# The last stage of a fused transformer-like block on one core: routing put beside the next pair's first logits, gate term held in PSUM, outputs written tile by tile

## The reference, cut to what matters

```
x = x + attention(layernorm(x), ctx)
x = x + lora_ffn(layernorm(x), ...)
h = layernorm(x)
x = x + (mask * h * A_S1 + (1 - mask) * h * A_S2)      # channel attention, mask from ctx
h = layernorm(x)
logits = h @ router_weight.T + router_bias             # 64 experts
scores = softmax(logits);  topk_w = top 8 of scores
w_dense = scores where among the top 8, else 0
x = x + (h * sum(topk_w) + w_dense @ expert_bias)
```

## Time and profile before

| | us |
|---|---|
| median of 3 runs | 4076.12 |
| lowest, highest of the runs | 4073.73, 4076.64 |
| the profiled execution: time | 4075.54 |
| the profiled execution: span of its trace | 4074.0 |
| expert stage in that trace (first matmul at 3506.5) | 567.5 |

### The profile page before, as it was taken

One profiled execution on the slowest core, in us unless ns is written; L12 is line 12 of the kernel. 1 busy time (PEld: TensorE's weight loads), 2 busy tenths in 40 slices (PEclk: granted clock), 3 DMA queues, 4 the chain that ended last, 5 costly groups with the idle time before them and its releaser, 6 DMA issues. The chain is left out here.

```text
span 4074.0 us, 52120 instructions
## 1 busy us (share of the span) xinstructions
PE 3533.0 (87%) x14366; PEld 1876.7 (46%) x14366; DVE 2914.6 (72%) x6957; ACT 1990.7 (49%) x5301; POOL 1740.0 (43%) x1103
## 2 busy tenths in 40 slices
PE   5999999999999995999999989989999960377777
PEld 3666666666666663444443434444444430122222
DVE  3777777777777763368888897879798887365654
ACT  4445444544454431445646474655655553443431
POOL 4777767767777662003131311304040313154544
PEclk9999999999999997999999999999999985677776
DMA  4333333333333224444536353545444431334342
GB/s 158 119 106 122 111 106 126 106 114 121 123 126 110 85 66 149 117 126 131 164 104 191 104 166 100 164 121 166 126 148 146 122 96 52 127 114 164 115 155 83
DMA packets 415676, 504.14 MB, mean 124 GB/s; under 512 B 19350, under 2 KB 349465, under 8 KB 392505
## 3 DMA queue, kind: packets, MB, share of 16 engines
q1 hardware_dynamic: 394076, 392.22, 30.9%
q10 hardware_dynamic: 9824, 71.34, 4.7%
q0 software_dynamic: 11520, 37.76, 2.8%
HBM read 370.16 MB, written 131.10 MB: 123 GB/s over the span
## 5 line engine op out<-in xcount | busy, mean ns | idle before, releaser
L887 PE MATMUL acc<-xh,ws 128*128 128x512 f16 x4096 | 1238.2, 390 | 87.7 <-DVE xr L1384 84.1
L887 PE MATMUL acc<-xl,ws 128*128 128x512 f16 x2048 | 775.7, 388 | 3.4 <-DVE xl L1191 3.4
L887 PEld LDWEIGHTS acc<-xh,ws 128*128 128x128 f16 x4096 | 406.3, 100 | 644.5 <-issue 132.4
L1041 ACT ACTIVATE unused<-ct,minus_guess 128x256 bf16<-128x256 f32 x1024 | 505.1, 494 | 342.1 <-DVE minus_guess L1259 254.5
L796 POOL DMA_DIRECT2D ct<-ctx_pairs x128 | 71.1, 556 | 1044.6 <-DVE mk L1309 1035.2
L390 PE MATMUL bu<-m_iz,zf 128*128 128x256 f32 x2048 | 457.2, 382 | 11.8 <-issue 11.8
L390 PEld LDWEIGHTS bu<-m_iz,zf 128*128 128x128 f32 x2048 | 392.2, 192 | 94.0 <-issue 43.1
L887 PEld LDWEIGHTS acc<-xl,ws 128*128 128x128 f16 x2048 | 204.0, 100 | 260.0 <-issue 23.3
L316 POOL TENSOR_TENSOR xt<-xt 128x512 f32<-128x512 f32 x64 | 81.0, 1266 | 375.6 <-ACT xt L496 375.6
L409 PE MATMUL bx<-m_ic,pf 128*128 128x256 f32 x1024 | 234.3, 382 | 3.8 <-POOL pf L248 3.8
L358 PE MATMUL by<-cx,m_k 128*128 128x512 f32 x512 | 231.6, 595 | 2.6 <-DMA cx<-ctx 2.6
(11 more groups left out here) (260 smaller groups left out, 7522.6 us busy)
## 6 DMA issues: line engine op xcount, KB each, us to landing
ws<-w_split SPq DMA_DIRECT2D x128, 1024.0 KB, 5.4
xn<-x SPq DMA_DIRECT2D x16, 2048.0 KB, 7.6
cx<-ctx SPq DMA_DIRECT2D x64, 512.0 KB, 5.1
xt<-xT SPq DMA_DIRECT2D x64, 512.0 KB, 3.9
x_pairs<-xo SPq DMA_DIRECT2D x64, 512.0 KB, 3.2
ct<-ctx_pairs POOLq DMA_DIRECT2D x128, 256.0 KB, 3.7
xn_pairs<-xr ACTq DMA_DIRECT2D x32, 1024.0 KB, 4.8
x<-xn_pairs SPq DMA_DIRECT2D x32, 1024.0 KB, 4.9
```

The costliest lines, as they stand in the source:

```text
L887: product = lambda k, a, x, start: pe.matmul(acc[b][:], ws[o % WR][:, k, a, :], x[:, k, :], start=start, stop=False)
L1041: act.activation(signs[:, u // 2, t] if n == COUNTS - 1 else unused[u % 2][:], ct[k % CR][:, t], ACT.Sign, bias=guess[q % 2][:, u:u + 1], ...
```

## The change

Only `experts_phase` is changed.

1. `x3` is done in halves (128x1024) and its sum goes to a PSUM tile `up` and no longer back to `gc`. The multiplication then reads one operand from PSUM and one from SBUF.
2. The ring `po` has 3 buffers of one tile (128x512); biases and outputs go tile by tile, 16 instructions a pair on DVE for 8 before. The PSUM tiles `tr` and `ab` become one, `rw_ps`, which also takes the transposed weights.
3. The first two chunks of the *next* pair's `x3` are made early on DVE: two halves among the outputs, two within `routing`. PE does the logits of those chunks and the squares of chunk 0 between the transposes of `lgs` and `weights`.
4. The order on PE is a row of small groups (3 biases, 2 squares, 4 logits, and so on), and ACT squares chunk 0 and 1 of the next pair before `weights`.
5. There are 3 buffers `sq`, and POOL halves chunks 0 and 1 of the next pair after the products.
6. SP loads `xr` of the next pair chunk by chunk, each behind the products that used its buffer, and stores a chunk of the pair before after each load, one pair earlier in its program than before.

The diff, cut to what sets the order:

```diff
-    RING = 2
+    RING = 3
-        sq = [sb(f"sq3_{i}", [P, CK, T]) for i in range(2)]
+        sq = [sb(f"sq3_{i}", [P, CK, T]) for i in range(NCH - 1)]
-        lw, tr, ab, dev = pb("lw", [P, 512]), pb("tr", [P, 512]), pb("ab", [P, 512]), pb("dev3", [P, 512])
-        po = [pb(f"po{i}", [P, HK, T]) for i in range(RING)]
+        lw, rw_ps, dev, up = pb("lw", [P, 512]), pb("rw_ps", [P, 512]), pb("dev3", [P, 512]), pb("up", [P, HK, T])
+        po = [pb(f"po{i}", [P, T]) for i in range(RING)]
...
@@ SP, pair(i, s, u)
+                for c in range(NCH):
+                    if not is_last(i):
+                        if least(i, 1):
+                            n_used = counted(sp, NH * (i - 1) + CH * (c + 1))
+                            sp.wait_ge(k_in, 96)
+                            sp.wait_ge(prod_ok, n_used)
+                        load_x(i + 1, 1 - s, c)
+                    if least(i, 1):
+                        n_out = counted(sp, KT * (i - 1) + CK * (c + 1))
+                        sp.wait_ge(k_in, 96)
+                        sp.wait_ge(out_ok, n_out)
+                        store(i - 1, c)
...
@@ POOL
             def pair(i, s, u):
-                for c in range(NCH):
-                    halve(i, c)
+                for h in range(NH):
+                    if h in (2, 5):
+                        halve(i, 2 + h // 4)
                     if least(i, 1):
-                        products(i, 1 - s, c)
+                        product(i, 1 - s, h)
+                if not is_last(i):
+                    halve(i + 1, 0)
+                    halve(i + 1, 1)
...
@@ PE
+            def bias(i, s, u, k):
+
+                if k >= RING:
+                    pe.wait_ge(out_ok, KT * (i - 1) + k - RING + 1)
+                elif least(i, 2):
+                    pe.wait_ge(out_ok, KT * (i - 1))
...
+                pe.matmul(po[(KT * s + k) % RING][:], eb[:, k * P:(k + 1) * P], wds[s][:], start=True, stop=True).then_inc(bias_mm, 1)
...
+                biases(0, 1, 2)
+                squares(i, 1)
+                logits(i, s, 2)
+                biases(3, 4, 5)
+                logits(i, s, 3)
+                if not is_last(i):
+                    deviation(i + 1, 1 - s, u + s)
+                squares(i, 2)
+                biases(6, 7, 8)
+                squares(i, 3)
+                biases(9, 10, 11, 12, 13, 14, 15)
+                pe.wait_ge(lg_ok, i + 1)
...
                 for q in range(QT):
                     mm = pe.transpose(raw[:, q, :], lgs[:, q * P:(q + 1) * P], ident[0:A, 0:A])
                 mm.then_inc(tr_mm, 1)
                 if not is_last(i):
-                    deviation(i + 1, 1 - s, u + s)
-                if least(i, 1):
-                    biases(i, 1 - s, u + s - 1, 2)
-                    biases(i, 1 - s, u + s - 1, 3)
+                    logits(i + 1, 1 - s, 0)
+                    logits(i + 1, 1 - s, 1)
+                    squares(i + 1, 0)
                 weights(i, s)
...
@@ ACT, pair(i, s, u)
+                squares(i, s, 2)
+                if follows:
+                    act.wait_ge(mk_in[1 - s], 16 * (u + s + 1))
+                    gates(i + 1, 1 - s, 0)
+                squares(i, s, 3)
+                if follows:
+                    gates(i + 1, 1 - s, 1)
+                act.wait_ge(lg_mm, i + 1)
...
+                act.activation(lgs[:], lw[0:A, :], ACT.Copy).then_inc(lg_ok, 1)
+                if follows:
+                    gates(i + 1, 1 - s, 2)
+                    squares(i + 1, 1 - s, 0)
+                    gates(i + 1, 1 - s, 3)
                 act.wait_ge(var_ok, i + 1)
                 act.activation(r4[:], r4[:], ACT.Sqrt, bias=eps[:]).then_inc(std_ok, 1)
                 act.wait_ge(arg_ok, i + 1)
                 act.activation(sc[:], lt[:], ACT.Exp).then_inc(exp_ok, 1)
+                if follows:
+                    squares(i + 1, 1 - s, 1)
                 act.wait_ge(wt_mm, i + 1)
...
@@ DVE
+            def x3(i, s, u, h):
+                c, k = h // CH, slice(h * HK, (h + 1) * HK)
...
+                dve.tensor_tensor(up[:], gc[c][:, h % CH * HK:(h % CH + 1) * HK, :], dev[:].unsqueeze(1).broadcast_to([P, HK, T]), ALU.add).then_inc(u_ok, 1)
...
+                dve.tensor_tensor(xr[s][:, k, :], up[:], xr[s][:, k, :], ALU.mult).then_inc(x3_ok, 1)
...
+                o = ost[k // CK][:, k % CK, :]
+                dve.tensor_tensor(o, o, po[(KT * s + k) % RING][:], ALU.add).then_inc(out_ok, 1)
...
                 dve.tensor_tensor(lt[:], raw[:, :, 0:E], lm[:], ALU.subtract).then_inc(step_ok, 1)
+                if not is_last(i):
+                    x3(i + 1, 1 - s, u + s, 2)
                 dve.wait_ge(step_ok, n + 4)
...
                 dve.tensor_tensor(lt[:], lt[:], bc(mx), ALU.subtract).then_inc(arg_ok, 1)
+                if not is_last(i):
+                    x3(i + 1, 1 - s, u + s, 3)
                 dve.wait_ge(exp_ok, i + 1)
...
+                x3(i, s, u, 4)
+                x3(i, s, u, 5)
+                x3(i, s, u, 6)
+                outputs(0, 1, 2)
+                x3(i, s, u, 7)
+                outputs(3, 4, 5, 6)
+                ahead(0)
+                outputs(7, 8, 9)
+                ahead(1)
+                outputs(10, 11, 12, 13, 14, 15)
+                routing(i, s, u)
```

More of the change, by code:

```diff
@@ L1847, in _ @@
             for k in range(KT):
[L1848 removed]
+                mm = pe.matmul(rw_ps[:, 0:E], ones[:], rt[:, k, 0:E], start=k == 0, stop=k == KT - 1)
             mm.then_inc(rsum_mm, 1)
@@ L1899, in pair @@
-            def pair(i, s, u):
-                for c in range(NCH):
-                    logits(i, s, c)
-                    if c:
-                        squares(i, c - 1)
-                    if c in (1, 2) and least(i, 1):
-                        biases(i, 1 - s, u + s - 1, c - 1)
-                squares(i, NCH - 1)
-                pe.wait_ge(lg_ok, i + 1)
-                if least(i, 1):
-                    pe.wait_ge(wd_ok, i)
+                pe.matmul(rw_ps[:], pick[0:A, :], wds[s][0:A, :], start=True, stop=True).then_inc(ab_mm, 1)
@@ new lines, in pair, with biases @@
+            def pair(i, s, u):
+                earlier = least(i, 1)
+                def biases(*tiles):
+                    if earlier:
+                        for k in tiles:
+                            bias(i, 1 - s, u + s - 1, k)
+                biases(0, 1, 2)
[10 more added lines that the diff above has]
+                pe.wait_ge(lg_ok, i + 1)
+                if earlier:
+                    pe.wait_ge(a1_ok, i)
@@ L1966, in weights @@
                     act.wait_ge(prod_ok, NH * (i - 1))
[L1967 to L1983 removed]
+                act.activation(a1[s][:], rw_ps[:], ACT.Identity, bias=ones[:, 0:1]).then_inc(a1_ok, 1)
             act.wait_ge(mk_in[0], 16)
```

187 lines of the change are left out of this document (77 added, 110 removed).

## The result

| | before | after |
|---|---|---|
| median, us | 4076.38 (4 runs) | 3940.98 (4 runs) |
| lowest, highest | 4073.73, 4078.88 | 3939.08, 3953.02 |
| the profiled execution: time, span | 4075.54, 4074.0 | 3939.08, 3937.5 |

The account below looks back on a forecast made before the run. No engine was full; each 68.4 us pair was a ring of waits, PE its largest part. 3567.0 (first pair) + 6 x 49 + 41 (last) + 36.8 (tail) = 3938.8 of span, so 3940 us; forecast range 3924 to 3955, chance 0.60.

Parts of the forecast that it names:

- PSUM gate term: In `x3` on DVE: the sum in PSUM removes the collision with POOL, so a half takes 2.5 us, not 3.5.
- the first pair: Start of the expert stage: ACT's gates and squarings set it, routing ends at 3567.0 us, no gain over 3566.4.
- (a): Routing's end to `weights`: four logits and two squares stand ahead on PE, 7.5 us from cold, so `weights` starts 2.9 later.
- (b): `weights`: PE comes to it warm, so it takes 2.4 us where it took 4.0 at 1.2 GHz.
- (c): PE from `weights` up to bias 6: 20 matmuls at 0.86 us, 17.2 us, with no lasting wait inside.
- (d): DVE from bias 6 to routing: ten outputs and two halves of `x3`, 12.0 us, the seven last biases keeping pace.
- (e): Routing on DVE with two halves of `x3` inside: 13.0 us and 0.1 of hand-offs, square root ready just in time.
- allowance for the clock: Added to each pair: 1.4 us, as three last biases at half clock cost 2.6, taken half the time.
- The first (no cold start): Rival: PE does not go cold in the routing gap; pair 45.3 us, total 3916; chance 0.08.
- The second (the clock falls again during `weights` and the first biases): Rival: PE falls to 1.2 GHz a second time each pair; pair 54.3 us, total 3977; chance 0.22.
- The third: Rival: DVE's collision with POOL stays; pair 51.6 us, last pair 43, total 3958; chance 0.05.
- The fourth: Rival: PE never regains full clock in its small groups; pair 76.4 us, total 4130, slower; chance 0.03.

Follow-up runs that it names:

- no_hole: The kernel after with deviation one group earlier, both `x3` halves placed around output 6, and ACT's last gates behind the exponential: 3933.92 us, ratio 0.965.
- after_again: The kernel after, unedited, timed again on the same chip beside `no_hole`: 3942.52 us, ratio 0.967.
- gate_sbuf: The kernel after with the sum of gate and deviation written back to its SBUF tile: 3973.13 us, ratio 0.974.
- early_dev: The kernel after with the next pair's deviation one group earlier on PE and its first `x3` half ahead of output 6 on DVE: 3942.84 us, ratio 0.966.
- no_hole_busy_pe: `no_hole` with three filler matmuls, results unread, ahead of PE's second group of logits: 3929.95 us, ratio 0.964.

## Why the prediction was right

The mechanism held: the gain is the order's. All pieces in the old order gave about 4 us, and a warm `weights` in the old order none. Taking the PSUM gate term out of the new order costs 25 to 32 of the 136 us, so some 100 are the order with the other pieces. Which of its moves gives how much was not separated, but for the place of `weights`.

That the total is right to 1 us is luck. In the profiled execution the first pair ended 7.6 us later than forecast, the six steady pairs took 5.3 us less, the last pair 3.0 less and the tail 0.5 less, and these nearly cancel.

By steps, from the timeline above, for the long and the short pair:

| step | predicted | pair to 3721.1 | pair to 3767.4 | mean of six |
|---|---|---|---|---|
| (a) end of routing to `weights` | 2.9 | 1.35 | 0.05 | 0.9 |
| (b) `weights` | 2.4 | 2.5 | 2.5 | 2.5 |
| (c) PE up to bias 6 | 17.2 | 17.5 | 17.6 | 17.5 |
| (d) DVE from bias 6 to routing | 12.0 | 14.2 | 11.7 | 12.8 |
| (e) routing with two halves | 13.1 | 14.3 | 14.4 | 14.4 |
| allowance for the clock | 1.4 | in (d) | in (d) | in (d) |
| sum | 49.0 | 49.8 | 46.2 | 48.1 |

**(a) and (e)** were each off, and the errors offset each other, in part from one cause. The six matmuls took 7.5 us in the pair that ended at 3671 (3665.11 to 3672.64), as predicted, with the clock back 4.7 us after their start (0.52 in the window from 3666, so 0.16 of its 4 us at full clock, and 1.00 in the next). But routing is 1.3 us longer than forecast, because of the select steps: 2.97 us for four where `no_hole` has 1.25. POOL halves a chunk beside them. The select steps stand behind the last half of `x3`, so routing ends 6.2 us behind that half and not 4.6, and since PE has its six matmuls at that time, `weights` waits less by as much. The rest of the miss in (a) is that PE idled less before the second group than the "some 5 us", 2.7 to 3.9 us in five of six pairs, and needed less than 7.5 us in those pairs. The prediction looked for the collision on `x3` and products only; its halving "beside routing" was to cost nothing. In one pair of the six, the one that ended at 3721, PE idled just 2.75 us before its second group of logits and did them in 3.65; in the five others they took 5.01 to 5.98.

**(c)** was right to 0.4 us, and DVE's wait of 5.95 and 6.05 for bias 6 was the "some 6 us".

**(d)** is where long and short pairs differ. The hole of 1.20 us before the last three biases, which wait for an output behind `ahead(1)`, is in all six. In the three long pairs the clock falls to 0.50 during it or within 0.5 us behind it, and the three biases take 5.04, 5.49 and 5.49 us; in the three short ones 2.84, 3.09 and 3.28. Over 2.74 at full clock that is 1.5 us a pair, where the allowance was 1.4: "three biases at half clock cost 2.6, taken half the time". That the sizes agree so well is luck too, since nothing in the prediction says when the clock falls. Long and short pairs alternate in this trace, but `after_again`, the same kernel, has 47.4, 49.6, 49.6, 49.2, 46.7 and 46.9.

**The PSUM gate term**: 2.5 for a half was right (1.225 and 1.224 and the hand-offs). By the rule of the Trainium skill (SBUF — State Buffer, "SBUF: two separate sides") an operation of VectorE with at most one input in SBUF stays clear of the port that it shares with GpSimd, and the trace agrees: 64 of 64 multiplications within 1224 to 1225 ns. The bound from above, 51.6 a pair, is the bare 47.6 with four halves at 1.0 each and leaves out the allowance of 1.4 that the forecast of 49 has. With it the bound is 53.0, and `gate_sbuf` gives 53.5. The content is different, though: the halves within routing are not held up (1.22 and 1.23 us in the pair shown), the two ahead of it are, by 1.9 and 1.4, and the rest is the second hole and the products (2704 ns for 2356).

**The first pair** was the largest miss: its routing ended at 3574.6, not at 3567.0. The stage began 2.8 us later (first matmul at 3509.3), which is no effect of the change: in `after_again` it began at 3506.4. The other 4.8 us are two terms. The square root is ready 3.2 us late: "8 chunks of gates and 5 squarings are 8 x 4.03 + 5 x 1.91" took ACT's work as unbroken, but ACT's copy into `lgs` waits 4.4 us for PE, whose last squares end at 3551.96, and the next pair's gates, squaring and table load come behind it. And from the root to the end of routing it takes 10.7 us for 9.1, the select steps beside POOL's halving again.

**The last pair** took 38.0 us for 41: `weights` was 0.7 late and not 2.9, and there was no hole, so that the allowance of 1.4 was not used. **The tail** was 36.3 for 36.8, its 16 biases 27.32 us again.

**The rivals.** The first (no cold start) is seen in one pair of six, where it is worth about 1 us, since routing is then last. The second (the clock falls again during `weights` and the first biases) had more right than its absence from the profiled trace says. There, the first transpose of `weights` to bias 6 takes 20.0 to 20.2 us in all six pairs, at full clock. But `after_again`, the same kernel, has it in one pair of six:

```profile
3672.00:3678.00 6.00, 6.00 (x9) 1.95 (x8) 5.83 (x7) 4.35 (x7) 5.75 (x3) 0.50 0.00 0
```

That pair needs 23.5 us up to bias 6, so 3.4 more. `early_dev` has a fall before bias 6 in two pairs of six, and `no_hole` in three. By its own terms (1.0, 0.5, 2.6 and 2.3) the second rival's pair would be 54.0 without the allowance or 55.4 with it, and not 54.3. The third needs `gate_sbuf`. The fourth is refuted for this kernel: with three single tiles in the ring, the groups of 2 to 4 matmuls from `weights` to bias 6 run at 1.00 in all six pairs. The Trainium skill (TensorE: Matmul & The Clock Gate, "A second HAM failure mode: psum-queue depth-cycling") has a clock that swings where matmuls cycle through PSUM banks. In the trace of the kernel after it does swing, but at two waits for DVE, the idle before the second group of logits and the hole, and not from group to group.

**Open**: what decides whether the clock falls, at the hole and behind `weights`; how much of the gain warm biases alone would give in the old order; and what bounds `no_hole_busy_pe`, in which no single wait was taken further. A version clearly better than the changed kernel was not found: 12.6 us, 0.3%, is the most.

## What to carry to other kernels

Where one engine works through a chain of small steps and another waits for it, put independent work of the next round on both sides of that wait, in the waiting engine's order ahead of what it waits for: that gave 3% here, where eight fillers that warm `weights` gave nothing and removing the collision next to nothing in the old order. An edit's worth depends on whether it is on the path, so measure it in the order that it is for (25 to 32 us in the new order, while all pieces together gave 4 in the old). After such a change four engines are near the path together, and a further move mostly hands the last place on: in `no_hole` some 16 us were gained in one step of the pair and most of them lost in two others. So compare step by step, and not only the total.

## What the hardware showed that was not expected

- A tiny DVE operation can wait for a whole GpSimd instruction. 128x4 elements took 1.96 and 2.28 us for 0.16, and 128x64 took 2.02 for 0.29, each beside a GpSimd addition of 2.35 us, with whose end it ended. The Trainium skill (SBUF — State Buffer, "SBUF: two separate sides") says that the shared port is held for a whole instruction; what counts is then how long the neighbour's instruction is, not one's own.
- The same hole of 1.20 us, after the same instructions, had the clock at 1.2 GHz behind it in three pairs (three biases in 5.04 to 5.49 us) and mostly at 2.4 GHz in three (2.84 to 3.28). In the same trace, after idle of 2.75 us four logits took 3.65 in one pair, and 5.01 after 2.70 us in another. The length of an idle gap alone did not decide it.
- Sixteen biases in the tail never raised the clock: they take 27.32 us at 1.2 GHz in both kernels, while logits that start cold (at 3665.11 in the kernel after) are at 2.4 GHz 4.7 us later.
